# Layer 1 of a two-layer graph network: rings of five pairs, messages three pairs ahead, weights read from SBUF

## What is computed

```
# layer 0
x_t = mlp2(x);  e_t = mlp2(edge_attr)             # leaky relu between the two products
aggregated = segment_sum(x_t[src] * e_t * dp_scale, dst)
x = layernorm(x + (norm(x + aggregated * res_w) * gamma + beta))
# layer 1
rel_w = einsum('rb,bio->rio', w_comp, weight)     # 8 relations from 4 bases
xw = einsum('ni,rio->rno', x, rel_w)
msg = xw[edge_type, src] * edge_weight
x = layernorm(x + relu(segment_sum(msg, dst) + h_bias))
```

## Time and profile before

| | |
|---|---|
| median of three runs | 4093.48 us |
| profiled execution | 4086.35 us, of it span 4084.4 us |
| GpSimd busy | 2982.1 us, 73% |
| TensorE matmul busy | 2235.3 us, 55% |
| VectorE busy | 1596.9 us, 39% |
| ScalarE busy | 497.7 us, 12% |
| layer 1, first gather to last | 2114.18 to 4067.24 us |
| granted TensorE clock in layer 1 | 0.53 of full speed |

### The profile page before, as it was taken

One profiled execution on the slowest core, in us unless ns is written; L12 is line 12 of the kernel. 1 busy time (PEld: TensorE's weight loads), 2 busy tenths in 40 slices (PEclk: granted clock), 3 DMA queues, 4 the chain that ended last, 5 costly groups with the idle time before them and its releaser, 6 DMA issues.

```text
span 4084.4 us, 33230 instructions
## 1 busy us (share of the span) xinstructions
PE 2235.3 (55%) x7468; PEld 1486.8 (36%) x7469; DVE 1596.9 (39%) x3527; ACT 497.7 (12%) x955; POOL 2982.1 (73%) x3193
## 2 busy tenths in 40 slices
PE   6866666766676666667754444444443444444343
PEld 6644444544445444444422222222222222222222
DVE  5533334444444444444533332233323333333334
ACT  3211112121221222222310000000000000000000
POOL 3677777777777777777737777777777777777776
PEclk8877777778887888887865555555555555555555
DMA  4111111222222222222211111111111111111111
GB/s 115 37 40 40 40 40 45 52 57 47 51 58 46 57 58 57 58 58 69 52 47 27 27 27 27 27 29 27 29 27 29 29 29 29 29 29 29 29 29 29
DMA packets 175812, 169.75 MB, mean 42 GB/s; under 512 B 83970, under 2 KB 111478, under 8 KB 175502
## 3 DMA queue, kind: packets, MB, share of 16 engines
q0 software_dynamic: 100096, 102.60, 13.2%
q1 hardware_dynamic: 74524, 64.38, 5.1%
q10 hardware_dynamic: 882, 0.13, 0.0%
HBM read 134.80 MB, written 32.10 MB: 41 GB/s over the span
## 4 chain that ended last, share of the span: by engine, by line
POOL 64%; issue 22%; PE 8%; DVE 3%; ACT 1%; DMA 1%; DVEq 1%; ACTq 0%; POOLq 0%; SPq 0%
POOL rows L526 64%; PE ps_agg L1270 2%; PE ps_fin L1353 1%; PE ps_o L1262 1%; PE ps_agg L1353 1%; PE ps_o L1164 1%; PE ps_z L1246 1%; PE ps_T L1342 1%; DMA rows<-node_table,acc 0%; PE ps_z L1156 0%; PE ps_x L1156 0%; ACT L593 0%; DVEq L898 0%; PE ps_o L1203 0%; DVE work L987 0%
## 5 line engine op out<-in xcount | busy, mean ns | idle before, releaser
L526 POOL DMA_INDIRECT rows<-rel_table,row_ix x1564 | 1476.7, 944 | 537.4 <-issue 476.3
L526 POOL DMA_INDIRECT rows<-node_table,acc x1524 | 1439.5, 945 | 478.3 <-issue 461.4
L1270 PE MATMUL ps_agg<-work 128*128 128x256 f32 x2348 | 904.4, 525 | 1128.2 <-DVE work L987 1111.1
L1270 PEld LDWEIGHTS ps_agg<-work 128*128 128x128 f32 x2348 | 543.5, 255 | 1412.7 <-DVE work L987 1314.2
L987 DVE TENSOR_TENSOR work<-rows,ps_o 128x256 f32<-128x256 f32 x782 | 326.9, 418 | 1483.1 <-DMA rows<-rel_table,row_ix 1030.4
L905 DVE TENSOR_TENSOR work<-ps_x,rel 128x1024 f32<-128x1024 f32 x392 | 478.8, 1221 | 328.4 <-issue 191.4
L1270 PE MATMUL ps_z<-work 128*128 128x256 f32 x392 | 192.8, 644 | 289.3 <-DVE work L987 289.3
L916 DVE TENSOR_TENSOR acc<-acc,ps_agg 64x128 f32 x1174 | 331.5, 282 | 36.6 <-PE ps_agg L1270 27.0
L962 DVE SCALAR_TENSOR_TENSOR hid<-ps_z,b1e_c,low 128x512 f32<-128x512 f32 x196 | 147.1, 751 | 500.2 <-ACT low L593 471.7
L1262 PE MATMUL ps_o<-W2e_d,hid 128*128 128x128 f32 x1564 | 320.0, 368 | 0.0
L1270 PE MATMUL ps_T<-work 128*128 128x256 f32 x388 | 190.3, 643 | 223.3 <-DVE work L987 223.3
(11 more groups left out here) (145 smaller groups left out, 1351.2 us busy)
## 6 DMA issues: line engine op xcount, KB each, us to landing
rows<-rel_table,row_ix POOLq DMA_INDIRECT x1564, 2.4
attr<-in_edge_attr_dram SPq DMA_DIRECT2D x39, 640.0 KB, 4.6
rows<-node_table,acc POOLq DMA_INDIRECT x1524, 2.4
rel_table<-acc SPq DMA_DIRECT2D x13, 1792.0 KB
node_table<-work SPq DMA_DIRECT2D x24, 128.0 KB, 2.0
out_dram<-x_sb SPq DMA_DIRECT2D x13, 224.0 KB
rel_table<-acc SPq DMA_DIRECT2D x7, 256.0 KB
x_sb<-in_x_dram SPq DMA_DIRECT2D x1, 768.0 KB, 5.9
```

Source lines behind the costliest of these rows:

```text
L526: nc.gpsimd.indirect_dma_start(rows[0:n, t % BODY, j, :], None, table, bass.IndirectOffsetOnAxis(ap=lists[0:n, t, j : j + 1], axis=0),).th ...
L1270: last = nc.tensor.matmul(bank[:, 0 : 2 * P], data[:, 2 * jj : 2 * jj + 2, :], hot[:, 2 * jj : 2 * jj + 2, :], start=(jj == 0), stop=(jj = ...
```

## The change

Layer 1 gets rings of five pairs, kept in a part of `acc` that layer 1 doesn't use: five slots of messages, five of one-hots, and five PSUM banks, one for a pair's two sums side by side. VectorE prepares pairs 0 to 2 first, and in step p the pair p + 3 (one-hot and both messages), before it adds both sums of pair p. The message reads its weights from SBUF (`enorm`) at an address that depends on the pair; ScalarE's copies and their semaphore are gone. TensorE tells VectorE of a pair's two sums once. TensorE's folds of a chunk stand behind the third pair of a half instead of between halves. The layer 0 functions are split off unchanged.

```diff
+        msg_ring = acc[:, 1, at_ring : at_ring + HALF * V * J * F].rearrange("p (r q f) -> p r q f", r=HALF, f=F)
+        onehot_ring = acc[:, 1, at_ring : at_ring + HALF * V * J * P].rearrange("p (r q n) -> p r q n", r=HALF, n=P)
...
-        sums = [[[ps_agg0, ps_agg1], [ps_agg0, ps_agg1]], [[ps_agg0, ps_agg1], [ps_z, ps_T]]]
+        sums = [ps_agg0, ps_agg1]
+        pair_sums = [ps_agg0, ps_agg1, ps_z, ps_T, ps_o[0]]
...
+        AHEAD = 3
...
-            def stage_weights(k, h, n):
-                nc.scalar.copy(
-                    ps_o[h][:, 0 : n * J],
-                    enorm[:, bass.ds(k * BODY, n), :].rearrange("p t j -> p (t j)"),
-                ).then_inc(weights_staged, 1)
...
+            def add_pair(p, u):
+                dve.wait_ge(scattered[1][1], count(p, 0, SUM_LEAD))
+                bank = pair_sums[u % HALF]
+                add_window(window_of(u % 2, 0), bank, 0).then_inc(added[1][0], 1)
+                dve.wait_ge(added[1][0], count(p, 0, ADD_LEAD[0]))
+                if width(p) == V:
+                    add_window(window_of(u % 2, 1), bank, 2 * P).then_inc(added[1][1], 1)
+                else:
+                    dve.sem_inc(added[1][1], 1)
...
+            def prepare(q, u):
+                main_one_hot(q, onehot_ring[:, u % HALF, :, :])
+                for v in range(width(q)):
+                    slot = u % HALF * V + v
+                    await_rows(1, q, slot)
+                    factor = enorm[:, bass.ds(q * V + v, 1), :].rearrange(
+                        "p t (j o) -> p (t j) o", o=1).to_broadcast([P, J, F])
+                    nc.vector.tensor_tensor(
+                        msg_ring[:, u % HALF, v * J : (v + 1) * J, :], rows[:, slot, :, :], factor, ALU.mult
+                    ).then_inc(msg_ready[1][v], 1)
...
             def step1(p, u):
-                q, n = p + 1, (u + 1) % TURN
-                span_of(q, n % 2)
+                span_of(p + 1, (u + 1) % 2)
+                if not is_fixed(p) or p + AHEAD <= LAST:
+                    prepare(p + AHEAD, u + AHEAD)
                 if not is_fixed(p) or p > 0:
                     dve.wait_ge(added[1][1], count(p, -1, ADD_LEAD[1]))
-                main_one_hot(q, n % 2)
-                message(1, q, n, 0)
-                add_sums(1, p, u, 0)
-                dve.wait_ge(added[1][0], count(p, 0, ADD_LEAD[0]))
-                if width(q) == V:
-                    message(1, q, n, 1)
-                add_sums(1, p, u, 1)
+                add_pair(p, u)
...
+            def scatter1(p, r):
+                pe.reg_load(further, control[0:1, bass.ds(p, 1), 0:1].rearrange("p o v -> p (o v)"))
+                for t in range(width(p)):
+                    pe.wait_ge(msg_ready[1][t], count(p, MSG_LEAD))
+                    of_tile = slice(t * J, (t + 1) * J)
+                    last = sum_by_target(
+                        msg_ring[:, r, of_tile, :], onehot_ring[:, r, of_tile, :], pair_sums[r], t * 2 * P)
+                last.then_inc(scattered[1][1], 1)
...
+            def half1(k, first):
                 for u in range(HALF):
+                    scatter1(first + u, u)
                     if not is_fixed(first):
                         pe.reg_add(lead, lead, 1)
+                    if u == AHEAD - 1:
+                        next_chunk(pe, done, limit, k, finish1)
```

More of the change, by code:

```diff
@@ L709, in _ @@
             remaining_chunks(act, copied, limit, finish0)
-            act.wait_ge(msg_ready[0][0], LAST + 1 + MSG_LEAD)
-            for h in range(2):
-                stage_weights(h, h, BODY)
             act.reg_mov(copied, 0)
[L716 to L726, removed]
+            with act.Fori(0, BODIES - 1) as i:
+                next_chunk(act, copied, limit, i + 1, lambda c: finish1(c, i + 1))
             remaining_chunks(act, copied, limit, lambda c: finish1(c, BODIES + 1))
@@ L888, in _ @@
             further = [dve.alloc_register(f"dve_further{r}") for r in range(2)]
-            x_done, shift, left, lead, landed, staged = (
-                dve.alloc_register(f"dve_{n}") for n in ("x_done", "shift", "left", "lead", "landed", "staged")
+            x_done, shift, left, lead, landed = (
+                dve.alloc_register(f"dve_{n}") for n in ("x_done", "shift", "left", "lead", "landed")
             )
@@ L964, in edge_hidden, with await_rows @@
                 ).then_inc(hid_ready, 1)
-            def message(l, p, u, v):
-                slot = u % HALF * V + v
+            def await_rows(l, p, slot):
                 if is_fixed(p):
@@ L973, in message @@
                     dve.wait_ge(gathered[l][slot], landed)
[L974 to L986, removed]
-                nc.vector.tensor_tensor(
-                    msg[:, u % 2, v * J : (v + 1) * J, :], tile, factor, ALU.mult).then_inc(msg_ready[l][v], 1)
+            def message(p, u, v):
+                slot = u % HALF * V + v
+                await_rows(0, p, slot)
+                if v == 0:
+                    dve.wait_ge(mm2_done, count(p, 0, MM2_LEAD))
+                factor = ps_o[u % 2][:, v * J * F : (v + 1) * J * F].rearrange("p (j f) -> p j f", f=F)
+                nc.vector.tensor_tensor(
+                    msg[:, u % 2, v * J : (v + 1) * J, :], rows[:, slot, :, :], factor, ALU.mult
+                ).then_inc(msg_ready[0][v], 1)
+            def prepare(q, u):
+                main_one_hot(q, onehot_ring[:, u % HALF, :, :])
+                for v in range(width(q)):
+                    slot = u % HALF * V + v
+                    await_rows(1, q, slot)
[4 more added lines that the diff above has]
+                    ).then_inc(msg_ready[1][v], 1)
             dve.wait_ge(s_pool, 6)
@@ L1124, in layer @@
                 dve.reg_mov(landed, TILE_GATHERS)
-                dve.reg_mov(staged, 1)
                 span_of(0, 0)
[L1127 to L1130, removed]
+                if l == 0:
+                    main_one_hot(0, onehot[:, 0, :, :])
+                    message(0, 0, 0)
+                else:
+                    for q in range(AHEAD):
+                        prepare(q, q)
                 with dve.Fori(0, LOOPS) as i:
@@ L1274, in sum_by_target, with further_sums @@
                 return last
[L1276 to L1283, removed]
+            def further_sums(l, p, data):
                 with pe.While(lambda: pe.snap(further) > 0):
@@ L1403, in _ @@
             pe.reg_mov(lead, 4)
-            def half1(h, first):
+            def half1(k, first):
                 for u in range(HALF):
-                    scatter(1, first + u, (h * HALF + u) % 2)
+                    scatter1(first + u, u)
                     if not is_fixed(first):
                         pe.reg_add(lead, lead, 1)
[L1411 to L1416, removed]
+                    if u == AHEAD - 1:
+                        next_chunk(pe, done, limit, k, finish1)
+            with pe.Fori(0, BODIES - 1) as i:
+                half1(i, i * HALF)
+            half1(BODIES - 1, LAST - HALF)
+            scatter1(LAST, 0)
             remaining_chunks(pe, done, limit, finish1)
```

54 lines of the change are left out of this document (33 added, 21 removed).

## The result

Slower by a quarter of a per cent: 4103.82 us (median of nine runs) against 4092.43 us (nine), ratio 1.0027 with a 95% interval of 1.0018 to 1.0036, that is +11.4 us (7.4 to 14.7). Forecast were +8.9 us and 4102.4. On two other chips of normal speed the same kernel was 16.6 us slower (ratio 1.0040, 1.0027 to 1.0054) and 9.6 us slower (1.0025, 1.0015 to 1.0034). The intervals of these three (7.4 to 14.7, 11.0 to 22.1, 6.1 to 13.9) overlap, so the times alone don't tell them apart; the traces do, and the experiments show most of what makes the difference. The kernel before was traced once, on the first chip; where a trace from another chip is compared with before, it is compared with that one.

What follows compares the result with a forecast made beforehand. Layer 1's GpSimd gather stream was taken as the bound. Tail +7.9 and pace +1.0 gave +8.9 us: 4086.35 profiled became 4095.3, and with 7.1 to the median 4102.4; range 4096 to 4112.

Steps and rivals of the forecast that it cites:

- GpSimd binds and waits for no message: Layer 1: the gather stream sets the time, GpSimd never waits for a message, the rest runs in its shadow.
- The tail, +7.9: Layer 1's end: chunk 12's finish and more pairs of adds delay the last add by 7.9 us (7.2 to 10.5).
- The pace, +1.0 with ends 0 and 25: Layer 1's gather stream: messages with two SBUF inputs stretch some gathers, 1.0 us in all, between 0 and 25.
- the form, 0.30 less d: Layer 1: a 0.42 us message starting d before a gather stretches it by 0.42 - d - 0.12 us.
- The shift by register work: Layer 1: address arithmetic between wait and message delays message starts by 0.08 us or more, leaving 0 to 3.5 us.
- early starts in the forecast: Layer 1 before: of 350 messages that waited for rows, 72 start 0.05 us or more before a gather, 106 start 0.02.
- rival B: Layer 1: two-SBUF messages stretch gathers in number, 5 to 25 us beside the tail, 4106 to 4126 us; chance 0.18.
- over 4 us would be B: Sign in the changed profile: a gather stream longer by over 4 us would mean rival B.
- over 2 us would prove that something I hold unchanged is not: Sign: layer 0, taken as unchanged, ending over 2 us away from before would refute that.
- Rival C: Layer 1's end: chunk 12's finish stays in the wait for rows, only adds remain, +2.9 us, 4096.4; chance 0.15.
- The 7.1 us between profiled execution and median: Whole kernel: median 4093.48 lay 7.1 us above the profiled 4086.35; added to the changed kernel's 4095.3 for 4102.4.

Runs made afterwards that it cites:

- third trace: Changed kernel run again without an edit on a third chip, against the kernel before: 4101.81 us, +9.6 us, ratio 1.0025.
- second trace: Changed kernel run again without an edit on another chip, against the kernel before: 4101.36 us, +16.6 us, ratio 1.0040.

## Why the prediction was right, and where it was off

- **GpSimd binds and waits for no message.** Right, in each kernel on normal chips. Being three pairs ahead gains nothing, since no message can be ahead of its rows.
- **The tail, +7.9.** Right in mechanism and nearly in size: +8.6. The chunk began 2.26 us behind tile 389's message (forecast 2.0), its gap of 1.12 and the last one-hot followed as forecast. The adds were taken with gaps of 0.75, 0.22 and 0.3; they are 1.14, 0.58 and 0.15. That is 0.45 more than forecast, the 0.15 for register work included, and in both longer gaps the queue loads window registers (above). The split is 4.9 for the chunk and 3.4 for the sums, against the forecast's 5.0 and 2.9; the last 0.3 lies behind the last add, where the forecast had nothing.
- **The pace, +1.0 with ends 0 and 25.** The mechanism was right, and so was the form, 0.30 less d; the limit is 0.05. Messages stretched gathers by 1.8 us in the first trace: 0.4 by two that had waited for rows, 1.5 by eight of the 47 that hadn't (the forecast had a fifth of some 60 at 0.12 each). The net is 0.6, because the norm's product stretches no gather in the new order, 1.2 us that the forecast didn't count. The shift by register work is real: one fused register step of 69 ns ahead of 380 messages. From the landing of a tile's rows to its message it is 0.16 us in the mean in all three traces of the changed kernel and 0.07 before, so the shift is 0.09, where I had estimated 0.08 or more. The counts of early starts in the forecast (72 and 106 of 350) are a little low: by the trace 74 messages start 0.05 or more before a gather and 117 start 0.02 or more.

```profile
L990 DVEq FUSED_REGOPS  x380: 69/69/75, 2152.8 to 4050.4; - x190
```

- **The term that was mis-sized** is the same one on another chip: net 0.6 us in the first trace and 1.2 in the third, but 8.0 in the second. There, rows land earlier. From a gather's start to the landing of its rows the traces have a median of 2.37 us in all four kernels of that chip, and 2.43 to 2.45 in before's, the first, and all of the third chip's; layer 0 has the same difference. From a tile's last gather to its message it is 2.54 us in the mean, where the first and third trace have 2.61 and 2.62. Before's trace has 2.51, so the net shift is 0.03 there and 0.09 to 0.10 in the two others. Laid over the starts of before's messages that waited for rows, a shift of 0.03 leaves 6 to 8 us and one of 0.09 leaves 0.5 to 1; such messages cost 8.0 us in the second trace and 0.4 in the first. I had treated landing as fixed. So rival B is a part of the truth on that chip (it was to decide at a net shift under 0.04), and no part of it on the two others. On the first chip the tail and the stretched gathers make 8.6 + 0.6 = 9.2 of the 11.4; the rest is inside the interval, and I can't attribute it.
- **Two signs that were to speak against the forecast showed up in the first trace.** The stream is 4.3 us longer, and "over 4 us would be B"; layer 1 begins 2.1 us later, and "over 2 us would prove that something I hold unchanged is not". The level of 947 instead of 944, which layer 0 has with an unchanged program, is enough for both: 3.5 us of the 4.3, and an estimated 3.4 in layer 0. The signs were drawn too tight for a difference between two executions; the count of stretched gathers is the sign that tells B.
- **Rival C** didn't occur; the run with the earlier chunk is how its tail would have looked, but with costlier sums (3.4 and not 2.9).
- **The 7.1 us between profiled execution and median** were carried over as a constant. If they are mostly the two levels of the gathers, the forecast of 4102.4 rested on both kernels spending most runs at the same level; the times fit that, but one trace of each can't show it. The changed kernel's profiled execution (4101.30, level 947) lay 2.5 under its median and not 7.1, and 6 over the forecast's 4095.3 for it. That the median was met within 1.4 us is in part luck: before's median of nine is 1.05 under the one that the forecast started from, and the difference was 2.5 larger than forecast.

The Trainium skill (SBUF — State Buffer, Who interferes with whom) has the rule that a two-SBUF-input VectorE instruction and a GpSimd instruction that reads SBUF block each other, whichever is second. Read with the measured limit, it fits both sides of the limit, sorted by d: for d over 0.05 the gather is held to within 0.12 us of the operation's end, and for d of 0.02 to 0.04 it is the message that grows, to 0.48. With one input in PSUM neither does.

## What to carry to other kernels

Before running a producer further ahead, see what releases it: where it is a transfer that another engine paces, the lead can only be taken from the consumer, and that backlog is paid once, at the end of the stream, along with every side job that the new order pushes behind the last arrival. Look at the tail by itself, and thin out the lead there (a lead of one pair throughout kept it at 17.6 us; thinning it at the end alone wasn't run). And where a GpSimd stream of indirect DMAs is the bound, keep one input of each VectorE operation in PSUM: moving an operand to SBUF to save a small copy on an idle engine put the bound within reach of VectorE, at 1.8 to 9.2 us in this kernel.

## What the runs showed of the hardware that was not expected

- A gather is sensitive to a two-SBUF-input operation in one instant only: the operation has to have started about 0.05 us or more before the gather, and holds it until 0.12 to 0.13 us before its recorded end. Operations of 0.42, 0.62 and 1.22 us follow the same line, up to 1.05 us in one gather.
- An effect of 0.25 us at most for each message changed from 0.4 to 8.0 us in sum, over the messages that waited for rows, between two chips, for 0.07 us of landing time (2.44 and 2.37 us).
- All gathers of an execution have a median of 944 or 947 ns, in both layers, on one chip even; from the start of one gather to the next it is 1.2493 against 1.2515 us in layer 0, and over the 3088 gathers of both layers that makes an estimated 7 us.
- One chip took 5123 us for the kernel that takes 4085 to 4092 on the others.
